# Macaron block on one core: additions moved behind the last tile, gathers moved ahead, VectorE's tiles in nested loops

## The reference

```
x = x + 0.5 * ffn(layernorm(x))
x = x + attn(layernorm(x))
x = x + 0.5 * ffn(layernorm(x))

ffn: scores = softmax(x @ gate.T)            # 32 experts in 8 groups
     keep the 3 best groups, then the 6 best experts of each token (weights normalized)
     y = sum over the 6 of weight * (silu(x @ w1.T) * (x @ w3.T)) @ w2.T    # inner width 128
     shared = silu(x @ sw1.T) * (x @ sw3.T) @ sw2.T                         # inner width 256, every token
     return y + shared
attn: linear attention with decay in chunks of 128 tokens, 16 heads of 16, rotary turn of q and k,
      gate, rms norm by head, output weights
```

## Time and profile before

| | us |
|---|---|
| median of 3 runs | 960.03 (955.77 to 972.37) |
| the profiled execution | 960.5 |
| its span in the trace | 958.7 |
| TensorE clock granted, mean | 0.893 of full |

### The profile page before, as it was taken

How to read it: one execution, slowest core, us unless ns; L and a number is a source line. 1 busy time by engine, 2 the same in 40 slices (tenths; PEclk the granted TensorE clock), 3 DMA queues, 4 the chain that set the end, 5 groups by cost and what they waited for, 6 DMA issues and landing times. The chain is left out here.

```text
span 958.7 us, 16120 instructions
## 1 busy us (share of the span) xinstructions
PE 772.8 (81%) x4554; PEld 609.0 (64%) x4555; DVE 513.0 (54%) x1439; ACT 358.5 (37%) x799; POOL 465.3 (49%) x487
## 2 busy tenths in 40 slices
PE   6895997999969789788889575686999995867486
PEld 6464885888847546576677374564888884645154
DVE  5774942434313537888887469672444431135274
ACT  3160443444424314465665224233444442322000
POOL 3005665553053335867754320655555406456884
PEclk9979898999988898999999755688999998887798
DMA  6862465643233463222220140233444413334524
GB/s 209 338 286 77 158 214 176 231 164 120 89 121 114 159 227 89 80 76 67 72 62 2 34 176 1 77 121 120 153 158 154 138 77 121 126 112 131 207 82 153
DMA packets 42358, 126.43 MB, mean 132 GB/s; under 512 B 8352, under 2 KB 16704, under 8 KB 39488
## 3 DMA queue, kind: packets, MB, share of 16 engines
q1 hardware_dynamic: 23872, 75.40, 20.7%
q0 software_dynamic: 18432, 50.36, 18.0%
HBM read 76.44 MB, written 49.28 MB: 131 GB/s over the span
## 5 line engine op out<-in xcount | busy, mean ns | idle before, releaser
L399 POOL DMA_INDIRECT back<-token_table,slots x192 | 186.7, 973 | 221.9 <-DVE slots L644 96.3
L911 PE MATMUL bank<-w,xt 128*128 x1024 | 260.7, 400 | 33.2 <-ACT xt L492 18.4
L911 PEld LDWEIGHTS bank<-w,xt 128*128 128x128 f32 x1024 | 196.5, 200 | 69.4 <-issue 44.2
L420 POOL DMA_INDIRECT back<-slot_table,combine x124 | 130.0, 1049 | 143.6 <-SPq L328 42.2
L690 DVE TENSOR_TENSOR mids<-mids,bank 128x256 f32<-128x256 f32 x128 | 53.8, 420 | 256.6 <-ACT mids L469 197.3
L931 PE MATMUL bank<-w,mids 128*128 x512 | 142.9, 405 | 4.5 <-DVE mids L697 2.6
L492 ACT COPY xt<-ring 128x256 f32 x256 | 91.5, 408 | 104.0 <-issue 75.9
L931 PEld LDWEIGHTS bank<-w,mids 128*128 128x128 f32 x512 | 93.2, 203 | 16.0 <-issue 7.1
L469 ACT ACTIVATE mids<-bank 128x256 f32<-128x256 f32 x128 | 49.0, 383 | 145.2 <-PE bank L911 87.8
L680 DVE COPY ring<-bank 128x512 f32 (+1 forms) x96 | 66.1, 689 | 46.6 <-PE bank L901 31.2
L923 PE MATMUL bank<-const,mids 128*128 128x128 f32 x256 | 52.6, 290 | 45.7 <-DVE mids L690 24.2
(11 more groups left out here) (209 smaller groups left out, 1070.9 us busy)
## 6 DMA issues: line engine op xcount, KB each, us to landing
slot_table<-gT SPq DMA_DIRECT2D x32, 512.0 KB
slot_table<-ey SPq DMA_DIRECT2D x32, 512.0 KB
w<-in_w SPq DMA_DIRECT2D x12, 1024.0 KB, 17.1
slot_table<-w SPq DMA_DIRECT2D x6, 1024.0 KB
token_table<-back SPq DMA_DIRECT2D x8, 512.0 KB, 2.9
back<-token_table,slots POOLq DMA_INDIRECT x192
x<-in_x SPq DMA_DIRECT2D x4, 512.0 KB, 5.7
turn_a<-in_turn SPq DMA_DIRECT2D x4, 512.0 KB
```

Of the source, the lines that this page charges most:

```text
L399: pool.indirect_dma_start(out=rows[q % RX][:, a * H:(a + 1) * H], out_offset=None, in_=table, in_offset=bass.IndirectOffsetOnAxis(ap=slots ...
L420: pool.indirect_dma_start(out=returned[g % len(returned)], out_offset=None, in_=y_table, in_offset=bass.IndirectOffsetOnAxis(ap=combine[:, ...
L911: last = nc.tensor.matmul(bH[u % 2][:, a * 2 * I:(a + 1) * 2 * I], xt[u % 2][:, a * H + k * P:a * H + (k + 1) * P], w13[:, bass.ds(expert[ ...
```

## The change

For VectorE, the pairs are 8 written out, a loop to pair 16, then two laps of the ring as a loop of two turns with an inner loop, and a loop for the rest. The laps are whole (NC = 54), so six more pairs are copied into the ring than were gathered; PE raises e_xp by 6 so that VectorE does not wait for them. No addition is interleaved any more. In the first FFN the 32 additions stand behind the last copy_mid; in the second all 96 stand there, between the products and additions of the shared experts.

For POOL, the list of places has 32 entries in the first FFN, which is all it needs; gather 21 and later wait until PE has done the up step of 56 pairs. In the second FFN it has 46 entries (28 in back, 12 in w13, 6 in w2); gather 28 waits for pair 48, and gathers 46 and later wait on s_add. POOL's wait for all stores and the first 8 gathers for attention now stand at the end of the FFN's block, ahead of the barrier, behind a new semaphore s_share, and go to memory of their own (first_back).

SP loads the shared experts' tokens ahead of its last four stores, in both FFNs, as soon as PE has done the up step of 56 pairs; in the second FFN as four DMAs of 512 KB into places of the ring. wqkv and wo lie in the ring in attention. The diff, cut:

```diff
+LAP = RR // 2
+NC = -(-NP // LAP) * LAP
+GONE = 6
...
                 if f == 0:
-                    returned = [part[:, i * H:(i + 1) * H] for part, n in ((back, NT), (s1, KS * TB // H))
-                                for i in range(n)]
+                    returned = [part[:, i * H:(i + 1) * H] for part, n in (
+                        (back, NT), (s1, KS * TB // H), (kept, 1), (ring, 4), (ring[:, over:], 2),
+                        (ring[:, SPAN + (NB % RR + 1) * P:], 5)) for i in range(n)]
                 else:
-                    again = w13[:, 3 * KS * TB:3 * KS * TB + KC * T]
-                    returned = [back[:, i * H:(i + 1) * H] for i in range(KEEP)]
+                    again = [ring[:, a:a + KC * TB] for a in (spare, spare + KC * TB, SPAN + spare, 0)]
+                    returned = [part[:, i * H:(i + 1) * H] for part, n in ((back, KEEP), (w13, GONE * WE // H), (w2, GONE))
+                                for i in range(n)]
...
 # SP
-                        turns = NQ // 2 // RY - (f == 0)
+                        turns = NQ // 2 // RY - 2
...
+                        sp.wait_ge(e_h, done + NQ - EDGE)
                         if f == 0:
-                            sp.wait_ge(e_h, NQ - EDGE)
                             sp.dma_start(area[...], columns_table[...]).then_inc(s_here, 16)
+                        else:
+                            for it in range(T // TB):
+                                sp.dma_start(again[it].rearrange(...), stored[:, it]).then_inc(s_again[it], 16)
+                        for it in range(turns, turns + 2):
                             for u in range(RY):
-                                store(turns, u)
+                                store(it, u)
...
                         if f == 1:
-                            sp.wait_ge(e_h, done + NQ)
-                            sp.dma_start(again, columns_table).then_inc(s_again, 16)
 # POOL
                                 g = n * NT + i
+                                if f == 0 and g == NT + KS * TB // H + 1:
+                                    pool.wait_ge(e_h, NQ - EDGE)
+                                if f == 1 and g == KEEP:
+                                    pool.wait_ge(e_h, done + GONE * NT // 2)
+                                    pool.wait_ge(e_yp, done + GONE * NT // 2)
                                 if g >= len(returned):
                                     pool.wait_ge(s_add, g - len(returned) + 1)
-                                if f == 0 and g % 2 == 0:
-                                    pool.wait_ge(e_h, NQ - NT - 3 + g // 2)
...
+                        if f == 0:
+                            pool.wait_ge(s_share, 1)
+                            pool.wait_ge(s_there, ST + 4)
+                            for j in range(RB):
+                                gather_rows(j, j)
 # VectorE
-                        pairs(0, EDGE, first=True)
-                        at, laps = EDGE, [n * RR // 2 - 2 for n in range(1, NB // RR + 1)] + [NP - 2]
-                        for end_of in laps:
-                            with dve.Fori(0, (end_of - at) // 2) as it:
-                                pairs(it * 2 + at, 2, at=it * 4 * P + (at + 2) % (RR // 2) * 2 * P)
-                            pairs(end_of, 2)
-                            at = end_of + 2
-                        with dve.Fori(0, (NQ - EDGE - NP) // 2) as it:
-                            pairs(it * 2 + NP, 2)
-                        pairs(NQ - EDGE, EDGE, final=True)
+                        pairs(0, EDGE, at=4 * P, first=True)
+                        dve.sem_inc(s_share, 1)
+                        with dve.Fori(0, (LAP - 2 - EDGE) // 2) as it:
+                            pairs(it * 2 + EDGE, 2, at=it * 4 * P + (EDGE + 2) * 2 * P)
+                        with dve.Fori(0, NC // LAP - 1) as lap_of:
+                            pairs(lap_of * LAP + LAP - 2, 2, at=0, wraps=True)
+                            with dve.Fori(0, LAP // 2 - 1) as it:
+                                pairs(lap_of * LAP + it * 2 + LAP, 2, at=it * 4 * P + 4 * P)
+                        with dve.Fori(0, (NQ - NC) // 2) as it:
+                            pairs(it * 2 + NC - 2, 2)
+                        pairs(NQ - 2, 2)
                         copy_mid(NQ - 1, NQ - 1)
+                        if f == 0:
+                            for n in range(EARLY):
+                                for i in range(NT):
+                                    add_row(n, i, (n - 1) * NT + i + 1, 2 * len(its))
-                            add_rows(2)
+                            add_rows(0, 0)
                             product(0)
-                            add_rows(3)
+                            add_rows(1, 0)
                             product(1)
-                            dve.wait_ge(s_add, 4 * NT)
-                            shared_of(0, 2)
-                            add_rows(4)
+                            shared_of(0, 2, 2)
+                            add_rows(2, 2)
                             product(2)
-                            dve.wait_ge(s_add, 5 * NT)
-                            shared_of(2, 4)
+                            shared_of(2, 4, 3)
                             product(3)
-                            add_rows(5, 0, NT // 2)
-                            shared_of(4, 8)
-                            add_rows(5, NT // 2, NT)
+                            add_rows(3, 4)
+                            shared_of(4, 8, 4)
+                            add_rows(4, 8)
+                            add_rows(5, 8)
 # PE
+                                elif more and q + 2 == NP:
+                                    pe.wait_ge(e_xp, read + NP)
+                                    pe.sem_inc(e_xp, NC - NP)
 # attention, POOL
-                        pool.wait_ge(all_there, ST + 4)
-                        for j in range(RB):
-                            gather_rows(j, j % B)
```

More of the change, by code:

```diff
@@ L186, in ffn @@
                     area, staged = (ring[:, a:b] for a, b in itertools.pairwise(at))
-                    back = [ring[:, b * REST * H:(b + 1) * REST * H] for b in range(RB)]
-                    assert RB * REST * H <= at[0] and at[-1] <= KC * SPAN
+                    first_back = mem.enter_context(nc.sbuf_tensor("first_back", [P, RB * REST * H], F32))
+                    back = [first_back[:, b * REST * H:(b + 1) * REST * H] for b in range(RB)]
+                    assert at[-1] <= KC * SPAN
                     back_ok = [ctx.enter_context(nc.semaphore(f"a_back{b}")) for b in range(RB)]
@@ L198, in gather_rows, with moe @@
                             ).then_inc(back_ok[j % RB], 16)
-                    all_there, shared = moe(f, combine, share, ring, area, sw13, sw2)
-                    attention(share, back, back_ok, gather_rows, all_there, shared, area, sw13, sw2, staged, ring)
-                else:
-                    moe(f, combine, share, ring, None, sw13, sw2)
-        def moe(f, combine, share, ring, area, sw13, sw2):
+                    shared = moe(f, combine, share, ring, area, sw13, sw2, first_back, gather_rows)
+                    attention(share, back, back_ok, gather_rows, shared, area, sw13, sw2, staged, ring)
+                else:
+                    moe(f, combine, share, ring, None, sw13, sw2, None, None)
+        def moe(f, combine, share, ring, area, sw13, sw2, first_back, gather_rows):
             with ExitStack() as mem:
@@ L247, in moe @@
                 top = sb("top", [P, NT * 8])
-                place, wts, equal = (back[:, NT * H + k * E16:NT * H + (k + 1) * E16] if f else sb(n, [P, E16])
-                                     for k, n in enumerate(("place", "wts", "equal")))
+                later = back[:, NT * H:] if f else first_back
+                place, wts, equal = (later[:, k * E16:(k + 1) * E16] for k in range(3))
                 mv, rs = sb("mv", [P, NT * 2]), sb("rs", [P, NT])
@@ L280, in moe @@
                 bX, bH, bG, bY = bank[0:2], bank[2:4], bank[4:6], bank[6:8]
-                done, read = f * NQ, f * NP
+                done, read = f * NQ, f * NC
                 def v3(ap, k):
@@ L715, in shares, with add_row @@
                             ch(nc.vector.tensor_reduce(v3(share[:, :], TOPK)[:, :, k], v3(equal[:, :], E), AX.X, ALU.add))
-                        def add_row(n, i):
+                        def add_row(n, i, before, shared):
                             k, g = TOPK - 1 - n, n * NT + i
@@ L723, in add_row @@
                                 dve.wait_ge(s_last[i // 4], NT // 4 * 16)
-                            if n:
-                                dve.wait_ge(s_add, g - NT + 1)
-                            if f == 0:
-                                dve.wait_ge(s_yc, 2 * len(its))
-                            elif n > 3:
-                                dve.wait_ge(s_yc, 2 if n == 4 else 4 if i < NT // 2 else 8)
+                            if begun(before):
```

(22 more changed lines are left out.)

50 lines of the change are left out of this document (27 added, 23 removed).

## The result

The changed kernel takes **1000.0 us**, median of four runs (997.5 to 1002.0); the kernel before, run beside it, 964.6. The ratio is **1.040** (95% interval 1.030 to 1.049): slower. Every ratio here leaves out runs that are more than 1.5% above the fastest of their kernel (here one of 972.4; further down, among others, ones of 1101 and 4043 of the kernel before, and 1003.2 and 1004.7 of b_serial), so it is not quite the ratio of the medians of all runs. By the profiled executions the span is 1000.2 against 958.7, +41.5, where +29.8 was forecast.

The account below looks back on a forecast made before the run. No engine fills the span, so each edit was judged by its stage: tail +14.1, tokens 0, second FFN's tiles 0, first FFN's +1, barrier +14.7, sum +29.8 on 958.7, forecast 990 us; own range 977 to 1004, over all 956 to 1003.

Parts of the forecast that it names:

- the barrier: Between first FFN and attention: additions, a held gather and seven more open it 17.8 us later; 3.1 comes back, +14.7.
- the tail: Second FFN, behind the last tile: 50 gathers remain instead of 41, and five runs of additions hold gathers; +14.1 us.
- the second FFN's tiles: Last pairs of the second FFN, beside bursts of gathers: 0 us taken, between -6.2 and +8.8.
- the holds: A gather beside a run of 16 additions lasts until the run ends: 4.3 us first, then 2.8; 15.5 in the tail.
- One sign: In the tail of the profile after: TensorE done some 10 us before the end.
- no holds: Rival: the two new places of additions, behind the tiles and at the barrier, hold no gathers; 967 us, 12%.
- The price by length: Second FFN's tiles: each burst of gathers costs its length less 8 us; +5.7 or +8.8 us.
- One price per burst: Rival, second FFN's tiles: the burst of 30 gathers costs what the 16 did, 11.9 us; -13.8, total 976; 20%.
- The tiles of the first FFN: Two more gathers in the first burst, then 11 in a burst as before; +1 us (-5 to +4).
- The shared tokens: Second FFN: coming early, they take 12.3 us out of TensorE's chain, which POOL's chain covers; counted as 0.
- VectorE's loops: Six more copies of 0.69 us into the ring in each FFN cost nothing; uncovered it would be 8.3 us.
- VectorE's written-out code: Rival: this straight code, not gathers, makes ScalarE stand still; loops take most losses away, 953 or 938 us; 10%.

Follow-up runs that it names:

- b_serial: Kernel before, with each row addition in the second FFN waiting for the one right ahead of it: 985.4 and 999.5 us against 964.6, on the slower chip.
- x_serial: Changed kernel, with each row addition waiting for the one right ahead, leaving small gaps: 878.2 us, 0.994 of the kernel before, on the faster chip.
- x_tokens: Changed kernel, with the second FFN's shared tokens loaded behind the last store again: 893.5 us, 1.012 of the kernel before, on the faster chip.

## Why the prediction was right or wrong

The forecast, 990 with a range of its own up to 1004, held: 1000.0, slower, and the barrier and the tail are the two largest terms, as said. The span grew by 41.5 instead of 29.8; most of the difference lies in the second FFN's tiles, which were put at nothing. That the barrier and the tail came out near their numbers is partly luck, since errors in them cancelled.

*The tail, second FFN.* Right to 1.4 us. From the first addition behind the tiles to the end it is 85.2 us against 72.4: +12.7, forecast +14.1. 46 gathers were out and 50 remained, as said. Three runs held a gather for 3.65, not five for 4.3 and 2.8; the last gather starts 72.6 behind the first, so the holds cost 10.6 beside 62.0 of pitches, not 15.5. What I had too small is the end: it comes 11.8 behind the last gather's start instead of 8.5, because VectorE's last additions of shared results were themselves late (9.79 us, "remote") and 32 row additions were still ahead of it. Holds 4.9 too long and an end 3.3 too short nearly cancel. One sign was also off: TensorE was done 38 us before the end, not "some 10"; the prediction's own terms give 35 (8.3 before the change, 12.3 sooner, the end 14.1 later).

*The holds.* This was the disputed rule, and the rows decide it. On both chips a gather beside an unbroken run of additions lasts until some 0.8 us behind the run's end, up to 7.93 us in all (343.99 to 351.92, the run ends at 351.09), and additions at a pitch of 0.57 instead of 0.40 us let the gathers in (x_serial). The rival "no holds" falls. "SBUF — State Buffer", section "Who interferes with whom", in the Trainium skill has the shared pair held for one instruction. The trace does not agree with a limit of one addition, 0.40 us; no run here shows whether it is that pair that holds the gather.

*The barrier.* Forecast +14.7, measured +17.4 (A) and +16.5 (B). The hold (7.93) and the seven pitches are as predicted. Two things were not foreseen. POOL's block closes 4.7 us behind its last gather (360.65 to 365.37; on B 320.6 to 325.35), where I had 0.3; before, that was hidden because POOL had long been idle at the barrier. And of the 3.1 us that I gave back behind the barrier only 0.6 came: the late products took 13.20 us instead of 10.54, at a granted clock of 0.80 instead of 1.00, so the transpose came 16.5 behind the barrier and not 14.0. Against these 6.9 us stand 1.4, since the additions ended 14.5 behind gate 63 and not 15.9, and 2.7 that attention was shorter from the transpose to the second FFN's gate 0 (255.9 instead of 258.6 us), for which I have no cause.

*The tiles of the second FFN.* This is the failed term: 0 was taken between -6.2 and +8.8, and it is +8.2 from gate 47 to the last copy_mid and +11.0 between the gates, outside my bounds. The price by length, with my 8 us free in each burst, was the nearer of the two and still too small (bursts of 19.9 and 36.2 us without a pause give 11.9 + 28.2 = 40.1 us lost, where 48.6 were). "One price per burst" falls with it: with the burst of 16, pairs 47 to 54 take 39.2 us instead of 22.3, and the burst of 30, a part of which lies ahead of pair 54's gate, cost the other 31.7. My bounds came from four bursts of near equal length, so they could not tell the laws apart, and half-way between was not a neutral choice. What makes ScalarE stand still stays open, and a part of the loss may be TensorE's clock: it was granted 0.69 from 844 to 884, beside the burst of 30, and 1.00 in the same stage on B (746 to 801).

*The tiles of the first FFN.* Forecast +1 (-5 to +4), measured +3.9 on A. The larger effect, VectorE's wait for rows with 20 places, I did not see at all; its end shows on B as -10.6.

*The shared tokens and VectorE's loops.* Tokens 0, as predicted, shown on B by x_tokens; on A TensorE was done 38 us before the end. The loops' six extra copies left gates 0 to 47 within 0.5 us in all but one stage (+1.1). The rival that VectorE's written-out code causes the standstills falls: with the loops they stayed on A, and on B the written-out code of the kernel before has none.

## What to carry to other kernels

Where GpSimd's indirect DMAs are the chain that sets the end, count them by their pitch from the first one, and keep long unbroken runs of VectorE's two-input additions away from them, or break them up. Do not put gathers between the last tile and a barrier: each cost its pitch of 1.265 us here, the close came 4.7 us behind the last, TensorE's idle 22 us were followed by a lower granted clock, and the rows were not needed that early. And look whether a gain was measured beside a loss that belongs to one chip: the same edit, gaps between additions, gave 1.3% of the changed kernel on one chip and cost 2 to 4% of the kernel before on another.

## What the runs showed of the hardware that I had not expected

Two kinds of chip differ by 9% on the same program (965 against 884 us), at nearly the same granted clock over the whole (0.893 and 0.919 in the two profiles of the kernel before). Half of the 77 us between these profiles lies in the last sixteen pairs of the second FFN (88.5 against 50.1); the first FFN's tiles, the second's and attention are slower on A too. The difference is in the trace: on A nine waits of ScalarE's gate, 54.8 us in all, have a releaser that the profile calls "remote". Eight of the nine begin while POOL is in an unbroken burst of 10 or more indirect DMAs, of tokens or of rows that come back. In the ten profiles on B no engine has such a wait, though POOL runs up to 96 of them with no pause over 0.6 us. What the slower chip's engines wait for in a burst, and whether a limit on the length of bursts would free them, stays open.
